# A two-layer transformer block on one core: who issues the stores of the heads' outputs in the first attention stage

## The reference, cut to what matters

```python
x = x + _L0_attn_ref(_layernorm(x), Wq, bq, Wk, bk, Wv, bv, Wo, bo, rel_emb)
# inside: q, k, v of shape (b, h, n, 8)
sim = jnp.einsum('bhid,bhjd->bhij', q, k) + bias[rp_bucket] * SCALE + causal
attn = jax.nn.softmax(sim, axis=-1)
out = jnp.einsum('bhij,bhjd->bhid', attn, v)
return out.transpose(0, 2, 1, 3).reshape(b, n, d) @ Wo.T + bo
```

## Time and profile before

| | |
|---|---|
| median of 3 runs | 1755.63 us (1755.18 to 1757.66) |
| the profiled execution | 1758.26 us, span 1756.3 us |
| mean granted TensorE clock, as a share of full speed | 0.944 |
| first attention loop, about 62 to 486 us of the span | 424.00 us |
| in it busy: PE, DVE, ACT, POOL | 384.18, 357.44, 328.97, 344.56 us |
| queue q1: packets, share of 16 DMA engines | 119178, 31.6% |
| queue q10: packets, share of 16 DMA engines | 432, 0.0% |

### The profile page before, as it was taken

How to read it: one execution, slowest core, us unless ns; L and a number is a source line. 1 busy time by engine, 2 the same in 40 slices (tenths; PEclk the granted TensorE clock), 3 DMA queues, 4 the chain that set the end, 5 groups by cost and what they waited for, 6 DMA issues and landing times. The chain is left out here.

```text
span 1756.3 us, 47346 instructions
## 1 busy us (share of the span) xinstructions
PE 1582.5 (90%) x18858; PEld 1007.6 (57%) x18858; DVE 1473.9 (84%) x2120; ACT 1260.3 (72%) x2523; POOL 810.2 (46%) x1480
## 2 busy tenths in 40 slices
PE   5699899899966999999899569999999999999965
PEld 3366666666665878877688324444444444444444
DVE  7688889898676999988676779999999999999834
ACT  6488778787843445444565748898888988889855
POOL 6488888888944010000340334444444444444445
PEclk9699999999966999999999869999999999999978
DMA  7522232323264756666000351111211121112031
GB/s 249 212 87 87 90 93 88 96 90 97 62 139 64 95 90 92 94 89 63 1 1 0 148 194 51 60 53 57 70 53 59 52 72 55 54 60 63 24 77 48
DMA packets 119828, 141.86 MB, mean 81 GB/s; under 512 B 22205, under 2 KB 80698, under 8 KB 119610
## 3 DMA queue, kind: packets, MB, share of 16 engines
q1 hardware_dynamic: 119178, 138.78, 31.6%
q10 hardware_dynamic: 432, 0.07, 0.0%
HBM read 92.70 MB, written 44.98 MB: 78 GB/s over the span
## 5 line engine op out<-in xcount | busy, mean ns | idle before, releaser
L952 DVE TENSOR_REDUCE heads_mx<-heads_psM 128x1 f32<-128x1024 f32 x512 | 602.5, 1220 | 39.7 <-PE heads_psM L1044 23.5
L1023 ACT ACTIVATE heads_probs<-heads_psS 128x512 f32<-128x512 f32 x1024 | 546.4, 601 | 75.0 <-PE heads_psS L1067 69.0
L647 DVE TENSOR_REDUCE heads_mx<-heads_psM 128x1 f32<-128x1024 f32 (+7 forms) x512 | 356.6, 752 | 57.2 <-PE heads_psM L778 43.4
L731 ACT ACTIVATE heads_probs<-heads_psS 128x512 f32<-128x512 f32 x576 | 310.2, 604 | 82.9 <-PE heads_psS L743 77.8
L690 POOL TENSOR_TENSOR heads_probs<-heads_probs,one_ebias 128x512 f32<-128x512 f32 (+2 forms) x320 | 314.4, 999 | 60.9 <-ACT heads_probs L731 54.3
L992 POOL TENSOR_TENSOR heads_masked<-heads_probs,g_tri 128x128 f32<-128x128 f32 x512 | 226.1, 456 | 232.1 <-ACT heads_probs L1023 232.1
L1044 PE MATMUL heads_psM<-three_kS,three_qS 48*128 48x512 bf16 x1024 | 229.6, 393 | 10.5 <-DVE heads_mx L952 6.7
L1067 PE MATMUL heads_psS<-three_qS,three_kS 50*128 50x512 bf16 x1024 | 237.1, 389 | 0.3 <-ACT heads_probs L1023 0.3
L1597 ACT ACTIVATE trees_hid_hi<-trees_hid 128x512 fp32r<-128x512 f32 x192 | 121.7, 634 | 152.0 <-DVE trees_hid L1618 151.2
L804 PE MATMUL heads_psS<-one_qS,one_kS 50*128 50x512 bf16 (+3 forms) x768 | 151.2, 338 | 28.0 <-DMA one_qS<-heads_mrow 26.3
L1618 DVE SCALAR_TENSOR_TENSOR trees_hid<-trees_psH,g_b,trees_chosen 128x512 f32<-128x512 f32 x192 | 143.9, 750 | 31.1 <-DMA trees_chosen<-leaf_choice 13.3
(11 more groups left out here) (273 smaller groups left out, 3153.4 us busy)
## 6 DMA issues: line engine op xcount, KB each, us to landing
trees_chosen<-leaf_choice SPq DMA_DIRECT2D x96, 256.0 KB, 7.3
head_outputs<-g_small SPq DMA_DIRECT2D x128, 128.0 KB
one_qS<-q_parts SPq DMA_DIRECT2D x128, 96.0 KB
one_kS<-k_parts SPq DMA_DIRECT2D x128, 96.0 KB
three_qS<-q_parts SPq DMA_DIRECT2D x128, 96.0 KB
three_kS<-k_parts SPq DMA_DIRECT2D x128, 96.0 KB
q_parts<-g_w SPq DMA_DIRECT2D x8, 768.0 KB, 4.1
k_parts<-g_w SPq DMA_DIRECT2D x8, 768.0 KB, 6.0
```

What stands on the lines that cost most here:

```text
L647: last = dve.tensor_reduce(mx[:, p, qb:qb + 1], psM[(n * NM + i) % 2][:, at:at + w], AXX, ALU.max, negate=True)
L731: act.activation(probs[n % 2][:, slot * CH:(slot + 1) * CH], ring.bank(i)[:, :], ACT.Exp).then_inc(slot_taken, 1)
L952: dve.tensor_reduce(mx[:, n % 2, k:k + 1], psM[k % 2][:, :], AXX, ALU.max, negate=True).then_inc(max_taken, 1)
L1023: act.activation(probs[n % 2][:, kb, h * CH:(h + 1) * CH], ring.bank(i)[:, :], ACT.Exp).then_inc(slot_taken, 1)
```

## The change

The store of a head's output is no longer issued by SP but by ScalarE, behind the exponential of unit 1, which is the first exponential after the copy. ScalarE waits for its own copy (`o_taken`) before it issues the store. The last two stores are issued by ScalarE behind the last copy. Nothing else changes: the same bytes, the same semaphores, the same order of everything else on every engine.

```diff
@@ SP's stream @@
-            def store_o(n):
-                sp.wait_ge(o_taken, n + 1)
-                hand.store_heads(sp, n)
-
...
                 hand.store_later(sp, n)
-                if n >= 2:
-                    store_o(n - 2)
                 if n + 1 < NG:
                     load_r(n + 1)
...
             for b in range(B - 1):
                 gather.load_inverse(sp, b)
-            store_o(NG - 2)
-            store_o(NG - 1)
@@ ScalarE's stream @@
+            def store_o(n):
+
+                act.wait_ge(o_taken, n + 1)
+                hand.store_heads(act, n)
+
...
                     if slot == 0 and n >= 2:
                         take_o(n - 2)
+                    if slot == 1 and n >= 2:
+                        store_o(n - 2)
             take_o(NG - 2)
             take_o(NG - 1)
+            store_o(NG - 2)
+            store_o(NG - 1)
```

## The result

The changed kernel takes 1765.25 us (median of 13 runs, 1763.33 to 1773.90) against 1757.30 us (median of 13, 1755.18 to 1763.74) for the kernel before. The ratio is 1.0055, with an interval of 1.0041 to 1.0069: it is slower by about 0.55%, 8 to 10 us. Its profiled execution has a span of 1765.2 us against 1756.3 us, at a mean granted clock of 0.943 against 0.944. The mean hides single heads in which the clock fell.

What follows compares the result with a forecast made beforehand. It took a chain through several engines, with `mrow`'s latency and its queue alternating, as the bound; +7.5 + 1.0 + 0.6 - 4.4 = +4.7 us on 1758.3 profiled or 1755.6 median gave about 1761 us, range 1742 to 1780.

Steps and rivals of the forecast that it cites:

- The delay on ScalarE: In each head, issuing the store after unit 1 makes unit 2 late by 0.26 us, bounds 0.1 to 0.72.
- The chain of the short head: `mrow` issue to first scores at least 2.80 us, then 2.95 us to the next issue: 5.75 us, no ScalarE slack.
- the first rival: In the loop, `mrow` no longer meets the store; two heads fall to the 12.02 us floor: faster, 1742 us, chance 0.2.
- Once in a pair of heads: In the loop, ScalarE's delay counts once per two heads, the queue covering the other: 29 x 0.26 = 7.5 us.
- The pair rule: In the loop to head 59, short and long heads alternate with a fixed sum, 12.56 us for two.
- The store leaves q1: With the store out of SP's queue, `mrow` gains 0.15 us per two heads, 29 x 0.15 = 4.4 us.
- The last four heads: With no queue in front of `mrow`, each pays the full delay: 4 x 0.26 = 1.0 us.
- The end of the loop: ScalarE issues both last stores behind the last copy; next phase starts 0.6 us later, the stores land no later.
- TensorE's wait: At a head's first scores, TensorE's wait for `mrow` should stay at about 40 us in total.
- The second: Rival: ScalarE stands still during the store's issue, delay 0.72 us per head, +25 us, 1781 us; chance 0.2.
- No difference: Rival: ScalarE's delay and `mrow`'s gain cancel, or the issue costs 0.1 us; within 3.5 us of 1756, chance 0.2.

Runs made afterwards that it cites:

- e8: Kernel before, stores still by SP, with ScalarE adding a short in-memory copy behind unit 1 of every head: 1.0062, 1767.93 us.
- e1: Changed kernel with the last three stores issued by SP again: 1.0063, 1770.09 us; run again, 1.0063, 1767.86 us.
- e10: Changed kernel with the store issued behind unit 6 instead of unit 1: 1.0396, 1826.88 us.
- e6: Kernel before with one-stride DRAM layouts for both loads and stores, stores by SP: 0.9818, 1727.63 us.
- e6a: Changed kernel (stores by ScalarE) with one-stride DRAM layouts for both loads and stores: 0.9799, 1723.68 us.
- e4: Kernel before with the stored outputs laid out so one store writes 128 rows of one stride, reloads split to fit: 0.9897, 1741.66 us.
- e5: Kernel before with `q_parts` and `k_parts` laid out so a load's 48 rows have one stride: 0.9822, 1727.92 us.

## Why the prediction was right

It said 1761 us, slower; 1765.25 us was measured. By its own steps:

- **The delay on ScalarE.** Right. Taken as 0.26 us, measured 0.23 us at unit 2 and 0.27 us at the copy of the rows. The issue took 0.53 us, not 0.58. SP issued 0.02 us behind the copy of the rows, as forecast. e8 shows that such a delay alone is enough for the loss.
- **The chain of the short head.** Mis-sized. I read "at least 2.80 us" from a head in which TensorE did not wait for `mrow`, and so gave ScalarE no slack there. The latency is 2.66 us, which leaves 0.14 us: the heads that were 5.75 us grew to between 5.85 and 5.88, by about 0.11 and not by 0.26 us. The floor of two heads in the first rival, 12.02 us, was too high for the same reason; two heads of 5.86 us are 11.72.
- **Once in a pair of heads.** The size fits, as far as it can be told. The pair rule gives 29 x 0.25 = 7.3 us with no gain; the four traces of this loop have +4.2 to +11.7 us, +7.3 on average. That the two agree to 0.1 us is luck, with such a spread and one trace of the kernel before. Nor was the strict alternation of long and short heads there to begin with: in the loop before, 25 of 57 heads are under 6.0 us, and three stretches have heads of 7.0 to 8.9 us. So the rule holds as a sum at best, and not head by head.
- **The store leaves q1.** Mis-sized. I took a gain of 0.15 us a pair, 4.4 us. The value had no row to stand on. With the loop's mean loss as large as the delay alone makes it, the gain is about nothing; it can't be told more closely than the loop's own spread allows. In the head looked at above, the store waits for the loads to pass and then still stands before `mrow`. This is the larger part of what the forecast missed. The rule of the Trainium skill that it weighed (DMA: Bandwidth & Descriptors, section on issuing engines not being separate DMA queues) gave no gain, and no run here shows one.
- **The last four heads.** Taken as 1.0 us; the copies of heads 59 to 61 moved apart by 0.5 us. Small either way.
- **The end of the loop.** Mis-sized: 0.6 us forecast, 1.53 us measured. The step that failed is "so they don't land later". I looked at the last two stores alone. The store of head 61 was ahead of SP's reloads before and is behind them now, and the last copy waits for it. e1 gives these stores back to SP, and the wait is gone.
- **TensorE's wait** was to stay at about 40 us and is 42.7 us.

In sum, 7.3 + 0.5 + 1.5 = 9.3 us of loss against the 8.9 us of the two spans and 8 to 10 us of the medians. The forecast of 1761 us was about half of that, +5.4 us on its 1755.6 (which came out as 1757.3 over more runs): right in the way and in the cause, low in the size.

The first rival (`mrow` no longer meets the store, faster) is refuted: the kernel is slower, its own rows show `mrow` still meeting the store, and e10 shows the small transfer standing behind the store though it is in another queue. The second (ScalarE stands still for 0.72 us) is refuted by ScalarE's timeline: the issue overlaps unit 1. "No difference" fell with the gain; e6 and e6a show that it holds where the store's issue lasts 0.33 us. What bounded the kernel, a chain through a few DMA engines, is shown by e4 and e5, which change only the layouts and the transfers that follow them: 1.0% and 1.8% faster, a part of which is the clock. How many engines a store uses was read from a share of 27.3%; with the new layout, 96 packets of a store pass in 0.40 us at a share of 69.0%, where before 76 took 0.80 us. The Trainium skill (DMA: Bandwidth & Descriptors, section on why a DMA increments its semaphore by 16) gives the rule that the slowest dimensions decide it; by that rule the new layouts take the store from 4 to 16 engines and the loads from 6 to 16. The share of 69.0% is more than 4 engines could reach, and the gains agree.

## What to carry to other kernels

Issuing a DMA is work of the engine that issues it. Before it is moved to another engine, look up whether that engine has slack just there: here an issue of up to some 0.3 us was free and one of 0.53 us cost 0.23 us in the chain that set the pace. If a small transfer is late behind big ones, another queue need not help; here it did not. The big ones' layout did: with rows of one stride the loads alone were worth three times what the change cost. Take a latency only from a place where the engine really waits for it: the 2.80 us here came from one where it did not, and hid 0.14 us of slack. And look at the loop's last rounds apart: an order of two issues that is harmless inside can come out the other way round there.

## What of the hardware was not expected

- How long ScalarE takes to issue a DMA depends on its shape: 0.25 us for 4 rows, 0.33 us for 128 rows of one stride, 0.51 to 0.53 us for 128 rows in 4 groups of 32, and 1.08 us for two of those.
- A small transfer (4 KB) in q1 waited for nearly the whole of a 128-row store in q10 that was issued just ahead of it: 95 packets of the store passed for one of q1. It made heads of 7.2 us where 5.8 to 6.8 us were usual, and the kernel 4% slower.
- After TensorE had waited 1.6 to 1.9 us for a transfer, the granted clock fell to 0.50 for about 7 us in the heads shown, and a head took 8.7 to 8.8 us. In the loops of e5 and e6 and of their kernels with the change, where these waits are nearly gone, it never fell.
- The pace of this loop differs by up to 7.5 us in 367 us between single executions of kernels that have the same instructions in it. A difference of 1.5 us, such as the end of the loop, can be read in a timeline there but not in the kernel's time.
